# A cross-attention and FFN block on one core: V before the last K, x statistics earlier, Wo's homes swapped, three last pairs in one form, masks by fused operations

## What is computed

```
x = x + tanh(g_xattn) * xattn(layernorm(x), ctx)        # x: 8 x 128 x 512, ctx the same
x = x + tanh(g_ffn)   * ffn(layernorm(x))
# xattn: q = rope(x @ Wq) with 32 heads of 128; k = rope(ctx @ Wk), v = ctx @ Wv with 8 heads, each
#   shared by 4 q heads; softmax(q k^T / sqrt(128), masked where the mask is 0) @ v, then @ Wo
# ffn: x12 = x @ w12^T + b12; (silu(first half) * second half) @ w3^T + b3, all 512 wide
```

## Time and profile before

| | |
|---|---|
| median of 3 executions | 699.14 us (698.04 to 699.17) |
| profiled execution | 698.85 us |
| its span, first to last instruction | 696.9 us |
| TensorE, VectorE, ACT, POOL busy | 668.4, 511.4, 321.9, 385.6 us |
| mean granted TensorE clock | 0.990 of full speed |

### The profile page before, as it was taken

One profiled execution on the slowest core, in us unless ns is written; L12 is line 12 of the kernel. 1 busy time (PEld: TensorE's weight loads), 2 busy tenths in 40 slices (PEclk: granted clock), 3 DMA queues, 4 the chain that ended last, 5 costly groups with the idle time before them and its releaser, 6 DMA issues.

```text
span 696.9 us, 10991 instructions
## 1 busy us (share of the span) xinstructions
PE 668.4 (96%) x3352; PEld 560.3 (80%) x3352; DVE 511.4 (73%) x839; ACT 321.9 (46%) x903; POOL 385.6 (55%) x323
## 2 busy tenths in 40 slices
PE   8988799889999999999999999999999999979998
PEld 7767688668888888888888888888888887868886
DVE  2468766588888888888888888888888887873433
ACT  4342631454545445555445454544554545865310
POOL 5555646596666655666665666665566644630000
PEclk9999899999999999999999999999999999999999
DMA  9977585423121222212132121213200142000002
GB/s 305 306 231 230 180 280 190 139 74 106 35 102 32 92 59 80 90 45 90 31 101 73 54 98 38 90 31 105 75 32 30 31 153 75 1 0 1 1 30 91
DMA packets 62155, 66.32 MB, mean 95 GB/s; under 512 B 5920, under 2 KB 43808, under 8 KB 62112
## 3 DMA queue, kind: packets, MB, share of 16 engines
q1 hardware_dynamic: 60688, 64.77, 28.9%
q0 software_dynamic: 384, 1.05, 0.5%
q10 hardware_dynamic: 1040, 0.00, 0.1%
HBM read 46.93 MB, written 18.87 MB: 94 GB/s over the span
## 4 chain that ended last, share of the span: by engine, by line
PE 82%; POOL 6%; DVE 4%; issue 3%; ACT 2%; DMA 1%; SPq 1%; POOLq 0%; DVEq 0%; ACTq 0%
PE f_bank L456 10%; PE o_bank L456 9%; PE o_bank L458 9%; PE o_bank L457 9%; PE f_bank L457 9%; PE f_bank L458 9%; PE s_banks L580 5%; PE t_bank L462 4%; PE pv_bank L458 3%; PE pv_bank L456 3%; PE pv_bank L457 3%; PE s_banks L581 2%; POOL k L1060 1%; PE s_banks L456 1%; PE s_banks L458 1%
## 5 line engine op out<-in xcount | busy, mean ns | idle before, releaser
L860 ACT ACTIVATE prob<-prob,small 128x128 f32<-128x128 f32 x256 | 99.7, 391 | 118.0 <-DVE small L1308 118.0
L1088 POOL TENSOR_TENSOR prob<-prob,small 128x512 f32<-128x512 f32 x64 | 66.7, 1042 | 147.9 <-DVE small L1316 147.9
L456 PE MATMUL o_bank<-wo_hi,o_hi 128*128 128x512 f32 x256 | 105.9, 414 | 1.4 <-issue 1.4
L456 PE MATMUL f_bank<-xT_hi,wq_hi 128*128 128x512 f32 x256 | 103.8, 405 | 0.9 <-POOL wq_lo L1044 0.6
L457 PE MATMUL f_bank<-xT_lo,wq_hi 128*128 128x512 f32 x256 | 100.6, 393 | 0.0
L458 PE MATMUL o_bank<-wo_hi,o_lo 128*128 128x512 f32 x256 | 100.5, 393 | 0.0
L458 PE MATMUL f_bank<-xT_hi,wq_lo 128*128 128x512 f32 x256 | 100.4, 392 | 0.0
L457 PE MATMUL o_bank<-wo_lo,o_hi 128*128 128x512 f32 x256 | 100.0, 391 | 0.0
L1044 POOL TENSOR_TENSOR q_lo<-q,q_hi 128x512 fp32r<-128x512 f32 x64 | 82.6, 1292 | 20.5 <-ACT q_hi L793 20.5
L1223 DVE TENSOR_TENSOR t_sin<-f_bank,rope 64x512 f32<-64x512 f32 x128 | 88.2, 689 | 2.8
L793 ACT ACTIVATE o_hi<-pv_bank 128x512 fp32r<-128x512 f32 x64 | 38.3, 598 | 106.7 <-PE pv_bank L458 106.6
(11 more groups left out here) (180 smaller groups left out, 1490.7 us busy)
## 6 DMA issues: line engine op xcount, KB each, us to landing
k_scratch<-ks_parts SPq DMA_DIRECT2D x16, 512.0 KB, 3.1
raw<-in_L_xattn_Wq_dram SPq DMA_DIRECT2D x32, 256.0 KB, 2.8
raw<-in_L_xattn_Wo_dram SPq DMA_DIRECT2D x32, 256.0 KB, 2.6
k_parts<-k_scratch SPq DMA_DIRECT2D x16, 512.0 KB, 3.4
v_scratch<-vs_hi SPq DMA_DIRECT2D x16, 256.0 KB, 3.8
v_scratch<-vs_lo SPq DMA_DIRECT2D x16, 256.0 KB, 3.9
v_hi<-v_scratch SPq DMA_DIRECT2D x16, 256.0 KB, 3.9
v_lo<-v_scratch SPq DMA_DIRECT2D x16, 256.0 KB, 4.3
```

The costliest lines, as they stand in the source:

```text
L456: nc.tensor.matmul(dst, st[0], mv_[0], start=start, stop=False)
L860: e = nc.scalar.activation(prob[:, k, h, :], prob[:, k, h, :], ACT.Exp, bias=nmin[k][:, h:h + 1], scale=-1.0, accum_out=psum_row[k][:, h:h ...
L1088: nc.gpsimd.tensor_tensor(prob[:, k], prob[:, k], rrow[k].unsqueeze(2).to_broadcast([128, GH, S]), ALU.mult).then_inc(pool_norm, 1)
```

## The change

- In `STAGE`, V blocks 14 and 15 now come ahead of K(7,0) and K(7,1), and Q2 and Q3 too. The copies and sums of the first pair are reordered to fit.
- The eight `x_stats` move from places 11 to 14 of the stage to places 3 and 4, the Newton steps from 14 to 9.
- The first group's Wo goes to `wo_hi`/`wo_lo`, which hold V's weights until V ends, and is split at place 31 instead of 36. Later groups take turns the other way round, and the FFN's first weights go to `cT_lo` and `wo_hi`/`wo_lo`.
- `late_pair` is gone. In `pair`, the next pair's first `scores` stands ahead of the last `pv`. Pair 28 has both its Q blocks; pairs 29 to 31 have none and are written out in one form.
- `mask_rest` is now four fused operations of 128 x 128 that add and take the minimum, in place of an add and a reduce over 128 x 512; `scores` waits for the whole mask before it.

```diff
-         ("K", 5, 0), ("V", 12), ("K", 5, 1), ("Q", 0), ("K", 6, 0), ("Q", 1), ("V", 13), ("K", 6, 1), ("Q", 2),
-         ("K", 7, 0), ("Q", 3), ("K", 7, 1), ("V", 14), ("V", 15), ("Q", 4)]
+         ("K", 5, 0), ("V", 12), ("K", 5, 1), ("Q", 0), ("K", 6, 0), ("Q", 1), ("V", 13), ("K", 6, 1), ("V", 14),
+         ("V", 15), ("Q", 2), ("Q", 3), ("K", 7, 0), ("K", 7, 1), ("Q", 4)]
...
-             17: [16], 18: [17], 21: [18], 25: [19], 36: [20, 21, 22, 23]}
+             17: [16], 18: [17], 21: [18], 25: [19], 31: [20, 21, 22, 23]}
...
-Q_LAST = {25: [56, 57], 26: [58, 59], 27: [60, 61], 28: [62], 29: [63]}
...
+        w12_hi = cT_lo
+        w12_lo = place("w12_lo", [128, KT, TOK], F32R, at["wo_hi"])
...
-                if p >= 25:
-                    return [q - 16 * gg for q in Q_LAST.get(p, [])]
+                if p >= PAIRS - 3:
+                    return []
...
-            hi, lo = (wo_hi, wo_lo) if odd else (wo1_hi, wo1_lo)
+            hi, lo = (wo1_hi, wo1_lo) if odd else (wo_hi, wo_lo)
...
-                    pe.wait_ge(dve_masked, 2 * n)
+                    pe.wait_ge(dve_mask, n)
...
                 pv(gg, c, 0)
                 prob_transpose(gg, c, 1)
                 out_proj(gg, c - 1, 1)
-                pv(gg, c, 1)
-                scores(gg, c + 1, 0)
-
-            def late_pair(gg, c):
-
...
                     pe.wait_ge(dve_rot, ROTS)
+                elif 8 <= t < 10:
+
+                    tiles_done(H_T + t - 8)
...
                 if b < 2:
-                    pe.wait_ge(act_fstage, 10 + (b == 0))
+
+                    pe.wait_ge(act_fstage, 7 + b)
...
 
+            scores(3, 5, 1)
+            out_proj(3, 4, 0)
             ffn_tile(0)
             ffn_tile(1)
+            prob_transpose(3, 5, 0)
+            out_proj(3, 4, 1)
+            pv(3, 5, 0)
+            prob_transpose(3, 5, 1)
+            scores(3, 6, 0)
+            ffn_tile(2)
+            pv(3, 5, 1)
+
+            scores(3, 6, 1)
             out_proj(3, 5, 0)
-            scores(3, 6, 1)
-            ffn_tile(2)
             ffn_tile(3)
             prob_transpose(3, 6, 0)
             out_proj(3, 5, 1)
             pv(3, 6, 0)
+            prob_transpose(3, 6, 1)
             scores(3, 7, 0)
-            prob_transpose(3, 6, 1)
             ffn_tile(4)
+            pv(3, 6, 1)
+
+            scores(3, 7, 1)
             out_proj(3, 6, 0)
-            pv(3, 6, 1)
-            scores(3, 7, 1)
             ffn_tile(5)
-            ffn_tile(6)
             prob_transpose(3, 7, 0)
             out_proj(3, 6, 1)
             pv(3, 7, 0)
+            prob_transpose(3, 7, 1)
+            ffn_tile(6)
             ffn_tile(7)
-            prob_transpose(3, 7, 1)
-            ffn_tile(8)
+            pv(3, 7, 1)
             out_proj(3, 7, 0)
-            pv(3, 7, 1)
-            ffn_tile(9)
-            ffn_tile(10)
-            out_proj(3, 7, 1)
             for b in range(4):
                 h_tile(b)
+            out_proj(3, 7, 1)
+            ffn_tile(8)
+            ffn_tile(9)
             tiles_done(H_T + 3)
             up(0, 0)
+            ffn_tile(10)
             ffn_tile(11)
...
-                act.wait_ge(pool_rope, KBLOCKS + 16 * gg + 4 * (c // 2) + 4)
                 if isinstance(n, int) and n < 2:
-
-                    act.wait_ge(pe_kq, ROT_ORDER.index(("K", 7, 1)) + 1)
+                    act.wait_ge(pool_rope, ROT_ORDER.index(("Q", 3)) + 1)
+                else:
+                    act.wait_ge(pool_rope, KBLOCKS + 16 * gg + 4 * (c // 2) + 4)
+                if isinstance(n, int) and n < 2:
+
+                    act.wait_ge(pe_kq, ROT_ORDER.index(("K", 6 + n, 1)) + 1)
...
                 if i == 34:
                     q_hi_copy(0, 0, 0)
+                if i == 35:
                     q_hi_copy(0, 0, 1)
+                if i == 36:
+                    exps(0, 0, 0)
                 if i and STAGE[i - 1][0] == "K":
...
+            q_hi_copy(3, 6, 0)
+            exps(3, 5, 0)
+            exps(3, 5, 1)
+            pT_hi_copy(3, 5, 0)
+            ffn_tile_copy(0)
+            q_hi_copy(3, 6, 1)
+            o_hi_copy(3, 5, 0)
+            pT_hi_copy(3, 5, 1)
+            ffn_tile_copy(1)
+            o_hi_copy(3, 5, 1)
+
+            q_hi_copy(3, 7, 0)
+            exps(3, 6, 0)
+            ffn_tile_copy(2)
...
+            h_norm(0)
+            h_norm(1)
             o_hi_copy(3, 7, 1)
...
             kk = r = 0
             for i, blk in enumerate(STAGE):
+                if i == 34:
+                    q_lo_split(0, 0, 0)
+                if i == 36:
+                    q_lo_split(0, 0, 1)
+                    norm(0, 0, 0)
                 if i and STAGE[i - 1][0] == "K":
                     k_lo_split(kk)
                     kk += 1
-                if i == 35:
-                    q_lo_split(0, 0, 0)
-                    q_lo_split(0, 0, 1)
-                if i == 36:
...
                 for what, b in TILES_AT.get(i, []):
                     if what != "rope":
                         tile_lo(what, b)
+                if i == 3:
+                    for b in range(6):
+                        x_stats(b)
+                if i == 4:
+                    x_stats(6)
+                    x_stats(7)
+                if i == 9:
+                    inv_std(0, 8, 0)
+                    shifts(0, 8)
                 for s in SPLITS_AT.get(i, []):
                     if s in V_CHUNKS:
                         first_chunk(s)
-                if 11 <= i < 15:
-                    x_stats(2 * i - 22)
...
                 n = n_of(gg, c, k)
-                dve.wait_ge(dve_masked, 2 * n + 1)
-                nc.vector.tensor_tensor(prob[:, k], s_parts[:, :, 0, :], prob[:, k], ALU.add).then_inc(dve_masked, 1)
-                dve.wait_ge(dve_masked, 2 * n + 2)
-                nc.vector.tensor_reduce(nmin[k], prob[:, k], mybir.AxisListType.X, ALU.min).then_inc(dve_mask, 1)
+                dve.wait_ge(dve_masked, n + 1)
+                dve.sem_inc(dve_go, 1)
+                for h in range(GH):
+                    op = nc.vector.tensor_tensor_reduce(prob[:, k, h, :], s_parts[:, h, 0, :], prob[:, k, h, :], 1.0, HUGE,
+                                                        ALU.add, ALU.min, nmin[k][:, h:h + 1])
+                op.then_inc(dve_mask, 1)
 
...
                 o_lo_split(0, 0, 0)
                 sin_q(6)
+                pT_lo_split(0, 0, 1)
                 cos_q(0, 7)
                 sin_q(7)
-                pT_lo_split(0, 0, 1)
...
-            h_stats(2)
+
+            o_lo_split(3, 6, 1)
+            mask_first(3, 7, 1)
+            recip(3, 7, 0)
+            mask_rest(3, 7, 1)
+            h_stats(3)
+            inv_std_begin(0, 4, NEWTON_OPS)
+            newton_step(0, 4, NEWTON_OPS, 0)
+            pT_lo_split(3, 7, 0)
+            recip(3, 7, 1)
             add_out(3, 6, 0)
-            recip(3, 7, 0)
-            o_lo_split(3, 6, 1)
-            mask_scores(3, 7, 1)
-            pT_lo_split(3, 7, 0)
-            h_stats(3)
```

More of the change, by code:

```diff
@@ L22 @@
 MASKED = float(2.0 ** 100)
+HUGE = float(3.0e38)
 NEWTON = 3
@@ L673, in _ @@
                     pair(gg, c)
-            for c in range(1, 4):
+            for c in range(1, 5):
                 pair(3, c)
-            late_pair(3, 4)
-            late_pair(3, 5)
             def h_tile(b):
@@ L924, in first_pair @@
                 chunks = pair_chunks(0, 0)
-                exps(0, 0, 0)
+                split_chunk(*chunks[0])
                 pT_hi_copy(0, 0, 0)
@@ L1005, in gate @@
                 hi(a_hi[:, m, :], t_sin[:, i % 2, :], act_ghi)
+            q_hi_copy(3, 6, 0)
[11 more added lines that the diff above has]
+            ffn_tile_copy(2)
+            exps(3, 6, 1)
+            q_hi_copy(3, 7, 1)
+            pT_hi_copy(3, 6, 0)
+            ffn_tile_copy(3)
+            o_hi_copy(3, 6, 0)
+            pT_hi_copy(3, 6, 1)
+            o_hi_copy(3, 6, 1)
+            exps(3, 7, 0)
+            ffn_tile_copy(4)
+            exps(3, 7, 1)
+            pT_hi_copy(3, 7, 0)
+            ffn_tile_copy(5)
+            o_hi_copy(3, 7, 0)
+            pT_hi_copy(3, 7, 1)
+            h_norm(0)
+            h_norm(1)
             o_hi_copy(3, 7, 1)
-            ffn_tile_copy(9)
-            ffn_tile_copy(10)
-            for b in range(4):
-                h_norm(b)
+            ffn_tile_copy(6)
+            ffn_tile_copy(7)
+            h_norm(2)
+            h_norm(3)
             for b in range(4):
                 h_copy(b)
+            ffn_tile_copy(8)
+            ffn_tile_copy(9)
             h_norm(4)
             h_norm(5)
+            ffn_tile_copy(10)
             ffn_tile_copy(11)
@@ L1114, in _ @@
                 for s in SPLITS_AT.get(i, []):
-                    if s not in V_CHUNKS and s < 20:
+                    if s not in V_CHUNKS:
                         first_chunk(s)
             def first_pair():
-                first_chunk(22)
+                chunks = pair_chunks(0, 0)
```

(24 more changed lines are left out.)

146 lines of the change are left out of this document (53 added, 93 removed).

## The result

The changed kernel takes 682.66 us (median of 4 executions, 682.45 to 682.95), the kernel before 699.11 beside it: ratio 0.9768, 95% interval 0.9752 to 0.9785, faster. Forecast 682.6.

What follows compares the result with a forecast made beforehand. TensorE, busy 668.4 of 696.9 us, was taken as the bound. 698.85 - 8.9 - 5.2 - 2.4, masks 0, gave 682.35, stated as 682.6 us because the profiled execution lay 0.3 below the median; range 678.5 to 688.5.

Steps and rivals of the forecast that it cites:

- A: Before the first x tile: earlier x statistics remove TensorE's 6.7 us wait and 2.2 us of half clock; -8.9 us.
- The clock part: TensorE at half clock from 74.65 to 79.1 us, after the wait for normalised x; costs 2.2 us.
- the POOL chain: POOL's sum for K(3,0), behind one chunk split, lets the first x tile be normalised at 66.4, margin 1.5 us.
- B: Between projections and first pairs: 4.7 us of waits shrink to about 1.2, 1.7 of half clock goes; -5.2 us.
- Just in time: POOL's work ends at T+10.9, TensorE wants first scores at T+11.1 (T: last V block's end); wait 0 to 0.3 us.
- rival 3: POOL's four Wo parts ahead of Q2 hold up the first scores, halving that gain: 685.2 us; chance 0.08.
- Fused masks: VectorE's four fused mask operations take 1.4 us as before, within the loop's margin; 0 us (0 to +0.3).
- Rival 1: The fused mask group runs serially, 2.1 us, costing only outside the loop: 685.7 us; chance 0.12.
- C: Last three pairs and FFN start: waits 6.6 us instead of 7.3, 1.7 of half clock gone; -2.4 us.
- nothing can be won, only lost: Inside the loop of pairs TensorE is busy 100.00 of 100.00 us at full clock, so no gain is possible.
- Rivals 2 and 5: 2: last pairs win nothing, 685 to 687 us, chance 0.15; 5: their waits are absorbed, -6, 679 us, chance 0.05.
- Rival 4: Fused operation slow on VectorE, making the kernel slower than before; at 1 us each, 732 us; chance 0.05.

Runs made afterwards that it cites:

- best2: Changed kernel with four repairs: earlier normalising of two x tiles, output-projection heads before late scores, last pair reordered, old score order in the loop; 679.03 us.
- again: The changed kernel unaltered, run once more beside other variants as yardstick; 682.67 us.
- pv_first: Changed kernel with the last probabilities-times-V ahead of the next scores again, only in the 24 pairs inside the loop; 682.17 us, ratio 0.9768.
- drag1: Changed kernel with the first add of the mask done twice in each pair's first batch; 689.61 us, ratio 0.9876.
- drag2: Changed kernel with the first add of the mask done three times in each pair's first batch; 708.66 us, ratio 1.0131.

## Why the prediction was right

The time and the bound were right: TensorE was, and stays, what the kernel waits for. That the total came within 0.1 us is luck, as the end of this section shows. By its steps:

**A, forecast -8.9.** Undoing costs 7.8, by the traces 6.5 to 7.1. The clock part was too large, 1.8 us rather than 2.2, and a wait of 0.7 to 1.4 us on xnorm stayed. So the step that failed is the POOL chain: I had the first tile normalised 1.5 us ahead of TensorE, and a wait of 1 to 3 us on xnorm was the sign I had named for it. VectorE's rotation of K(3,0) in the changed kernel, and POOL's timeline:

```profile
60.56 0.68 DVE L1246 SCALAR_TENSOR_TENSOR t_cos<-f_bank,rope 128x512 f32<-128x512 f32 x1
...
62.04 1.30 POOL L1060 TENSOR_TENSOR ks_parts<-k,ks_parts 128x512 fp32r<-128x512 f32 x1 [0.74 <-ACT ks_parts L795]
63.29 1.74 POOL L1060 TENSOR_TENSOR wk_lo<-raw,wk_hi 128x512 fp32r<-128x512 f32 x1
65.00 1.29 POOL L1076 TENSOR_TENSOR k<-t_cos,t_sin 128x512 f32<-128x512 f32 x1
```

and ACT's:

```profile
66.32 0.63 ACT L795 ACTIVATE ks_parts<-k 128x512 fp32r<-128x512 f32 x1 [2.01 <-POOL k L1076]
66.86 0.61 ACT L795 ACTIVATE wq_hi<-raw 128x512 fp32r<-128x512 f32 x1
67.38 1.50 ACT L836 ACTIVATE xnorm<-resid,small 128x512 f32<-128x512 f32 x2
```

I had reckoned 6.7 us from the end of K(3,0) to the first normalised tile (59.7 to 66.4). It took 9.5: the next block starts at 58.63, and the tile is done at 68.18. 1.9 us pass before the rotation starts, behind that of K(2,1) and a V part on VectorE. Then POOL, whose sum I had one chunk behind the rotation, still makes the low part of K(2,1), which I had left out, and a chunk of 1.74 us, not 1.29: the sum starts 2.4 us behind the rotation's end (62.64). ACT idles 2.01 us before the high part, with the shift long done. best2, with the normalising ahead of it, has no such wait. Places 3, 4 and 9 hid the statistics and the Newton steps as forecast: the steps end at 50.85, the rotation behind them starts at 51.37 where it was 49.57, and TensorE waits for nothing until the x tiles.

**B, forecast -5.2.** Undoing costs 5.7. Waits left: 0.20 us before the first scores (0 to 0.3 forecast), none for the norm (0.2), 0.59 before probabilities-times-V (0.4), and none that the view shows for the first mask of pair 1, 0.16 in `again` (0.6). "Just in time" held, rival 3 fell.

**Fused masks, forecast 0.** The term held (undoing costs 0.9, within its error of nothing), the duration did not: a step is 0.21 us, and the read costs nothing of it. VectorE's timeline in a pair of the loop:

```profile
289.90 0.69 DVE L1326 TENSOR_TENSOR prob<-s_banks,mfill 128x512 f32<-128x512 f32 x1
290.79 0.29 DVE L1335 CUSTOM_DVE_ANT_0 prob<-s_banks,prob 128x128 f32<-128x128 f32 x1 [0.20 <-DVE prob L1326]
291.00 0.08 DVE L1335 DVE_READ_ACCUMULATOR2_ANT small<- 128x1 f32 x1
291.00 0.28 DVE L1335 CUSTOM_DVE_ANT_0 prob<-s_banks,prob 128x128 f32<-128x128 f32 x1
```

The group is 0.93 us, and a gap of 0.20 is new ahead of it: 1.13 where I had 1.4. The minimum is there 0.3 us earlier: ACT waits 2.13 us for it in nearly every pair of `pv_first`'s loop, and 2.45 in the kernel before. Rival 1 (serial, 2.1 us) fell. The Trainium skill, page "VectorE: DVE Perf Modes", gives an estimate of 0.29 us for 128 elements by the formula of its errata section: the row agrees. Its section "The DRAIN you can't avoid" says that the next operation does not start until the pipe is empty, which I read strictly, but it adds that one that is not held starts earlier; the start 0.21 us behind an operation of 0.29 agrees with that.

**C, forecast -2.4.** Undoing costs 1.7. It is two things: 2.4 to 3.1 us saved at the end, where two of the three waits before scores were 0.84 rather than 1.3 (0.3 of it is the shorter group), the last pT_lo 1.46 rather than 1.0, the x tiles 0 rather than 0.6; and 0.7 us lost in the loop, where the text had "nothing can be won, only lost" and then reckoned no loss. Rivals 2 and 5 fell.

**Rival 4's price was too low.** Its break-even, 0.5 us of excess or a group of 2.9 us, counted each pair alike and neither the turns nor the clock. drag1 and drag2 stand 8.7 us below and 9.1 above the kernel before; between them a straight line gives a break-even at a group of about 2.2 us, my estimate; and the drags lengthen one mask of each pair, where a slow operation would lengthen both. There the turns of the loop and the last pairs pay, and the fused operation's 0.93 us was far from it.

The errors of A (+1.1 us), B (-0.5), C (+0.7) and the masks (-0.9) nearly cancel, and each is within what a total here can tell, or near it; the terms are less exact than the total looks. One execution also varies at its start: the first V block began at 15.81 us in `pv_first` and at 17.66 in `again`, in code that they share.

## What to carry over

Give every covered cost a margin of its own at each seam (first pair, loop turn, last pairs): an engine's loop turn is time that no row shows until a reorder brings the last operation of a pass close to the next one. When a step is moved earlier, ask what stands ahead of its reader on the reader's own engine, not only when its input is done. Where a wait can't be shortened, put a head of the accumulation behind it in front.
